# The query products of the gather loop, moved between the norms and the turned row marks

## What is computed

```python
xn = layernorm(x)
h  = xn @ W_layer.T + b_layer                       # gnn
v  = leaky_relu(a1[src] + a2[dst], 0.01)            # a1, a2: two products of h
att = softmax of v over the edges of one src row
gnn = segment_sum(att * h[dst], src)
q, k, v = elu(xn @ wq + bq) + 1, elu(xn @ wk + bk) + 1, xn @ wv + bv      # mix, 8 heads
mix = (q @ (k.T @ v)) / (q @ sum(k) + 1e-6) @ wo + bo
x = x + gnn + mix
weights = softmax((layernorm(x) @ W_x + b_x) @ W_slice + b_slice) / temp) # 8 heads, 64 slices
x = x + attention over the slices' tokens, spread back by the weights, @ W_out + b_out
```

## Time and profile before

| | |
|---|---|
| runs, median (lowest to highest) | 2304.6 us (2302.0 to 2306.59), 3 runs |
| the profiled execution, from its first to its last instruction | 2306.1 us |
| TensorE matmul / weight loads | 1454.6 us (63%) / 1093.9 us (47%) |
| VectorE | 1270.9 us (55%) |
| GpSimd | 1004.7 us (44%) |
| ScalarE | 677.9 us (29%) |
| granted TensorE clock, mean | 0.798 |
| the gather loop | from about 456 to about 2190 us |

### The profile page before, as it was taken

The page is one execution under the profiler, slowest core; times in us unless marked ns, Lnnn a source line. Parts: engine busy times, 40 slices in busy tenths (PEclk is TensorE's granted clock), DMA queues, the critical chain, the costliest instruction groups (busy, mean ns, idle before and its releaser), DMA issues. The chain is left out here.

```text
span 2306.1 us, 27679 instructions
## 1 busy us (share of the span) xinstructions
PE 1454.6 (63%) x8420; PEld 1093.9 (47%) x8420; DVE 1270.9 (55%) x4043; ACT 677.9 (29%) x1884; POOL 1004.7 (44%) x1126
## 2 busy tenths in 40 slices
PE   5599995355745655655655656656646547465889
PEld 3477874234534434434434434434434435344667
DVE  8978783154644644644644545545545535445744
ACT  0243441042322322322322323323323323223310
POOL 1167676535445445445345345345344354453000
PEclk8799997577778877778878778778777777787999
DMA  8011213223223223223223222222232232221064
GB/s 178 29 47 48 62 50 90 71 58 88 70 70 87 69 69 86 69 73 84 68 73 83 68 76 80 68 77 79 65 83 77 62 87 68 69 77 55 14 193 153
DMA packets 112593, 177.17 MB, mean 77 GB/s; under 512 B 35998, under 2 KB 84509, under 8 KB 112445
## 3 DMA queue, kind: packets, MB, share of 16 engines
q0 software_dynamic: 43184, 109.96, 18.0%
q1 hardware_dynamic: 52847, 44.64, 7.5%
q10 hardware_dynamic: 16414, 20.81, 2.9%
HBM read 139.68 MB, written 35.65 MB: 76 GB/s over the span
## 5 line engine op out<-in xcount | busy, mean ns | idle before, releaser
L1134 POOL DMA_INDIRECT big<-node_table,rest x825 | 784.9, 951 | 239.9 <-issue 225.9
L1220 PE MATMUL psum<-big 128*125 128x257 f32 x1700 | 399.2, 388 | 39.4 <-DVE big L1757 39.1
L1220 PEld LDWEIGHTS psum<-big 128*125 128x125 f32 x1700 | 316.2, 191 | 93.9 <-DVE big L1757 46.1
L1575 DVE TENSOR_SCALAR rest<-psum,rest 128x125 f32<-128x125 f32 x100 | 30.1, 344 | 594.8 <-remote 554.1
L1239 PE MATMUL psum<-rest 65*125 65x512 bf16 x52 | 34.6, 666 | 488.6 <-ACT big L1376 488.6
L1132 POOL TENSOR_TENSOR rest<-rest 1x1 f32<-1x1 f32 x100 | 18.9, 189 | 693.7 <-PE psum L1220 668.0
L1370 ACT ACTIVATE rest<-big,rest 128x125 f32<-128x125 bf16 x850 | 268.9, 493 | 134.2 <-DVE rest L1705 134.2
L1239 PEld LDWEIGHTS psum<-rest 65*125 65x125 bf16 x52 | 9.2, 176 | 521.2 <-ACT big L1376 521.0
L1376 ACT COPY big<-psum 128x250 f32<-128x250 f32 x52 | 19.1, 367 | 687.1 <-remote 682.5
L1241 PE MATMUL psum<-rest,big 128*125 128x512 f32 x208 | 177.5, 1005 | 0.0
L1757 DVE TENSOR_SCALAR big<-big,rest 128x125 f32<-128x125 bf16 x850 | 169.0, 281 | 0.0
(11 more groups left out here) (430 smaller groups left out, 2786.7 us busy)
## 6 DMA issues: line engine op xcount, KB each, us to landing
big<-node_table,rest POOLq DMA_INDIRECT x825
slice_weights<-rest ACTq DMA_DIRECT2D x51, 252.0 KB
big<-slice_weights SPq DMA_DIRECT2D x50, 252.0 KB, 3.8
node_table<-big SPq DMA_DIRECT2D x50, 126.0 KB
normalised_turned<-big SPq DMA_DIRECT2D x50, 125.0 KB
rest<-normalised_turned SPq DMA_DIRECT2D x50, 125.0 KB
out_dram<-rest ACTq DMA_DIRECT2D x50, 125.0 KB
X<-in_x_dram SPq DMA_DIRECT2D x1, 5600.0 KB
```

The costliest lines, as they stand in the source:

```text
L1134: pool.indirect_dma_start(Gt[:, u, q * TW:(q + 1) * TW], None, table, bass.IndirectOffsetOnAxis(ap=item[:, u, 2 * q:2 * q + 1], axis=0)).t ...
L1220: mm = pe.matmul(bank[bAgg][0:R, 0:D + 1], P[:, u, q, :], Gt[:, at, q * TW:q * TW + D + 1], start=q == 0, stop=q == Q - 1)
```

## The change

`queries(i+2)` no longer stands between `tokens(i)` and `mix(i+1)`. It is called between `norms(i+1)` and `turn(i+1)`. It gets a wait for the first addition of `add_sums(i)` (semaphore `s_agg`), since its products now overwrite columns of bank 4 before that item's sums start; the first call, ahead of the loop, has no such wait.

```diff
-                    def queries(m, v, k):
+                    def queries(m, v, k, first=False):
 
                         pe.wait_ge(xn_here[v], 16 * (k + 1))
+                        if not first:
+                            pe.wait_ge(s_agg, SA * (m - 2) + 1)
...
                         logits(i)
                         norms(i + 1)
                         if ahead:
+                            queries(i + 2, w, nv)
                             turn(i + 1, v)
                         sum_edges(i, u, odd, GROUPS[:3])
...
                         tokens(i, u)
-                        if ahead:
-                            queries(i + 2, w, nv)
                         mix(i + 1)
                         turn_y(i + 1, v)
 
-                    queries(1, 1, 0)
+                    queries(1, 1, 0, first=True)
```

## The result

The changed kernel takes 2335.9 us, the median of 4 runs (2328.7 to 2344.5), beside 2303.3 us (2292.7 to 2306.6, 4 runs) of the kernel before: a ratio of 1.0149, with a 95% interval of 1.0120 to 1.0178. It is slower, by 32.6 us, and no run of one kernel reaches into the range of the other; 2351 was forecast, in a range of 2289 to 2378. The profiled execution has a span of 2336.3 us.

The account below looks back on a forecast made before the run. No engine was full; a loop of waits bound the steps, each a gather burst plus 14.2 us GpSimd idle. 47 bursts x 1.0 us added 47 to 2306.1, making 2353, less 1.5 for the runs' median: 2351 us, range 2289 to 2378.

Parts of the forecast that it names:

- What it takes away: TensorE's row between tokens and mix: without the queries, mix and turned y are visible mid-burst; gain 0.4 us a burst.
- witness step: One step of the unchanged kernel's profile where turned y was read during the gather burst; GpSimd's idle 14.69 us against 14.04.
- The added wait: Queries' wait on the first addition of add_sums: satisfied when TensorE arrives; price 0, bounds 0 and 0.5 us.
- The queries in front of the sums: Queries add 1.05 us ahead of the sums, 2.07 at half clock; 1.0 us is covered by the wait for weights.
- rival A: Turned y stays behind the burst, clock unchanged; only 0.2 us a burst lost, 2314 us; chance 0.18.
- The clock: Early logits leave TensorE idle, so norms, queries, turns and first sums run at clock 0.50; 0 to 1.6 us a burst, 1.0 taken.
- upper value of 1.6 us a burst: Highest price per burst: 0.65 us for early turned y plus 0.95 for queries delaying the sums at half clock.
- of this case alone: Main forecast, early turned y and late clock: 0.45 to 1.6 us a burst, 2325 to 2378 us; chance 0.60.
- B: Turns still end before VectorE's first four weights, spread maxima read 0.4 us sooner: faster, 2286 us; chance 0.13.
- D: The change does nothing because hold and cover swallow all: 2305 us; chance 0.03.
- C: Late reads are TensorE's own backlog; 4 matmuls less release spread maxima 3.0 us earlier: 2164 us; chance 0.06.
- A burst of gathers holds back TensorE's late results: Others see TensorE's results after the sums only about 3 us after the burst's last gather, though recorded 14 us before it.

Follow-up runs that it names:

- the hold put in by hand: Kernel before, readers of turned y and spread maxima waiting until the gather burst landed: 2211.8 us beside 1612.8; three variants (turned y early, queries moved, both): 2263.4, 2231.3, 2288.8.

## Why the prediction was right, and where it was not

The direction, the mechanism and the range held. By its steps:

1. **What it takes away.** Turned y and mix did come early, in 37 of 46 bursts, as one witness step had shown. The gain was wrong in size: L1743 gained 0.75 us, not 0.4, although the witness's own rows showed 0.72 (3.92 us behind the last gather's start against 4.64). That is 16 us more over 47 bursts. The 0.4 was L1597's place in VectorE's row; where the rest comes from stays open. The 9 bursts with late turned y gained 0.46 too, and the hold put in by hand cannot show it.
2. **The added wait.** Price 0 holds: add_sums' addition (L1549, 1251.02) is done before the norms end, and the queries follow the norms at once.
3. **The queries in front of the sums.** In the step shown they took 2.05 us, the half-clock value, and the turns 2.02. They ate the wait for weights (39.1 to 4.3 us), as said. With late turned y their price was put at 0.2 us a burst (rival A) and was three times that: 0.64 by hand, 0.62 behind L1743 in the 9 late bursts of the trace after.
4. **The clock.** The direction held and both parts were too large. Half of the queries' push of 1.9 us, 0.95, was to arrive at GpSimd; by hand the push was 1.40 and 0.51 arrived. And early turned y was priced at 0.65 with its gain in it, from a single dear step: from L1742 to the next mark the witness takes 11.72 us, 1.37 more than the usual step; by hand, early turned y costs 0.97 to 1.10, and in the trace after 1.01. So the upper value of 1.6 us a burst became 0.81 in the 37 bursts that had early turned y. The forecast took 1.0 for all bursts, a value between its two bounds that no row gives; 0.69 was measured (32.6 / 47). With the terms as they stood, 1.6 a burst would have forecast 2380 us. That the forecast came as near as 15 us is in part luck: the middle value, and the 9 bursts that kept turned y late, hid most of the two errors.

Three of its figures don't follow from its own terms. 1.6 us a burst gives 2380 us at the top and not 2378; rival A with the gain of 0.4 gives 2295 and not 2304; and the 0.45 of the range "of this case alone" has no working. The outcome turns on none of them.

Of what was to show it: L1377 and L1598 ahead of the last gather's end, in 37 of 46 bursts; L1743 near 4 us behind that gather's start, 3.93; L1220 7.5 to 8.5 us behind L1743, 7.65; the clock at 0.50 until the turns, as the windows show, though it then rose, on the mean, just ahead of the first sums (7.32 us behind L1743) and not during them; GpSimd's wait near 715 us, 693.6, so it grew by 25.6 us where 47 were forecast. Rival A held in 9 of 46 bursts and fell in the others, B fell with L1220 at 7.65, D with the result. C wanted TensorE's late results to be a backlog of 3 us in 4 matmuls; they moved by 0.75, and L1743 stayed above C's 3.5 us.

What the prediction never questioned was its ground. "A burst of gathers holds back TensorE's late results" was read from one profile and taken as belonging to the kernel. On the two chips of the experiments it does not happen, and there the change gives 0.9877 and not 1.0149. That the execution of the result was one with the hold is nothing that the prediction had secured. The rule of the Trainium skill ("SBUF — State Buffer", Who interferes with whom), by which a DMA never contends with a compute engine, was weighed and set aside by rows. On the two chips of the experiments no row speaks against it (the queries are read 1.14 us behind their record with gathers running); in the first profile the late readers stay without an explanation.

## What to carry to other kernels

Where an engine's idle time lies decides as much as how long its row is: a result that is read earlier can pull work out of the stretch that kept TensorE's clock up, and the bill comes at the next dense stretch. Look at what runs directly ahead of the longest matmul row and keep it there; here one wait on ScalarE, with the queries left in their place, was as fast as the change where nothing is held back (1591.8 and 1593.1) and the fastest of the four under the hold (2211.8), so it is the version I would take; where the results are held back it was not run itself, but turned y is late there anyway. A wait whose releaser the profile can't name is a fact about that execution until another one, best on another chip, has shown it too: run the unchanged kernel elsewhere before building on it, and where a condition can't be had, put it in by hand and vary one thing at a time.

## What the hardware showed that was not expected

- The same program took 2303 us in the runs beside the result and 1613 to 1615 us on the two chips of the experiments. The gathers cost 0.95 us in both; the difference is when others see TensorE's results during a burst. The hold put in by hand accounts for 599 of 690 us. Whether it is the chip or something in its state at that time, and what the mechanism is, no run here shows.
- In the slow profile of before, TensorE's own spread maxima (L1210) stood idle 157.4 us in 127 pieces with "issue" as the reason; in the slow profile of after it was 13.3 us in 13, and the spread maxima were read late all the same (records done by 1232.3 in the step shown, read at 1247.69). So these idle pieces alone don't make them late.
- The last part of the kernel, which the change and the experiments do not touch, took 128.0 us at a granted clock of 0.995 in the profile of before and 135.5 us at 0.933 in that of after, and the four kernels with the hold by hand fall on the same two sides. A difference of some 8 us between two single profiles can be that alone.
- The granted clock of a whole dense row of sums followed idle gaps ahead of it: 24 records of the sums took 5.43 to 5.48 us, 6.73 (for 23), 7.44 or 8.47 us. The Trainium skill says in "TensorE: Matmul & The Clock Gate" (Loop structure matters more than you think) that the loop nest determines whether matmuls stay warm. In the four kernels the nest is the same, and one wait on another engine inside it was worth 51.5 us.
